# State-space stage: decays from ScalarE with a bias, the next batch's angles made early, two heads' values side by side, the batch loop unrolled

## The chip, the cores and the metric

The kernel runs on one core of a Trainium2 chip. Its time is device microseconds of that core. A core has TensorE (matmul, called PE; its weight loads are PEld), VectorE (DVE), ScalarE (ACT), GpSimd (POOL) and SyncE (SP), which issues DMAs. TensorE's clock has two levels here, 1.2 and 2.4 GHz; a row that says PEclk gives the mean share of 2.4 GHz that was granted.

## The reference

The program is a network of four layers, each `x = x + s * silu(g)`. Only the sequence mixer `s` of the last layer is touched, a state-space model with 8 sequences (batches) of 512 positions, 128 channels, 4 heads of 64 values and a state of 128. Cut to what matters:

```
z, x, Bg, Cg, dd_dt, dd_A, trap, angles = split(u @ W_in)
a  = min(-softplus(dd_A), -1e-4);  dt = softplus(dd_dt + dt_bias)
theta = cumsum(angles[:, :, None, :] * dt[..., None], axis=1)
K = rope(rmsnorm(Bg) * B_norm_w + B_bias, theta)      # per head
Q = rope(rmsnorm(Cg) * C_norm_w + C_bias, theta)
beta = sigmoid(trap);  ell = cumsum(a * dt)
y[i] = sum over j <= i of (Q[i] . K[j]) * exp(ell[i] - ell[j]) * weight(beta, dt)[j] * x[j]   # the chunked sum, whole
y = (y + D * x) * silu(z)
return y @ W_out
```

## The kernel before, in words

The stage is `ssm_phase`. It holds one batch (512 columns of `XN`, channels on partitions) at a time and runs the eight batches one after the other. Each engine has a program of its own; what orders them are semaphores, and within an engine the order is the written one. `i` is the batch, `h` the head, `jk` one of four blocks of 128 keys; the part of a head's 512x512 matrix with queries at or after block `jk` is 512, 384, 256 and 128 columns wide, packed by `KEYS_AT` into three rows of 512 columns (`dec`, `aw`, and banks 0 to 2 of `ps`).

For one batch, TensorE projects B and C (banks 0 and 1), the angles (bank 2) and B and C with their rotated halves swapped (banks 3 and 4); `out(i - 1)` makes the result of the batch before from `y`; then come the means of squares for the norms (`cst("mean")`, banks 5 and 6), the gate z (bank 7, twice) and the values x (banks 5 and 6, L2351). ScalarE squares (L2424), copies the angles out (L2427), takes logarithm and exponential for the norms (L2431, L2433), sine and cosine of the angles (L2435 to L2438), the values out of PSUM, adds the heads' biases (`biased`, L2449) and makes the gates. VectorE multiplies the angles by dt (L2515), sums them along the sequence (L2517), brings them within one turn (five instructions, L2520 to L2531), and norms (L2537, L2539).

Then the four heads. `spread(h)` (TensorE, L2363) copies cosine and sine of head h to the partitions that need them, banks 3 and 4. `prepare(h)` (VectorE) makes the two halves of the rotation, tiles `t2` and `t3` (L2553, L2555), and then the exponents of the decays, `dec = min(ellb - column, 0)`, in four instructions (L2564). `turned(h)` (GpSimd, L2478) adds the halves into `kq`. ScalarE takes the exponential of `dec` in place (L2462), and GpSimd multiplies the four diagonal blocks with a mask that holds the weights, `mm` (L2501; GpSimd makes `mm` at the start of each batch, L2487 and L2493). `products(h)` (TensorE, L2374) makes the 512x512 products Q.K in banks 0 to 2; `weigh(h)` (VectorE) multiplies them with `dec` into `aw` (L2577, L2580); `outputs(h)` (TensorE, L2383) multiplies the values with `aw` into banks 5 and 6, heads 0 and 2 into partitions 0 to 63, heads 1 and 3 into 64 to 127. After the last head VectorE multiplies with the gates into `y` (L2595).

Both `kq` and `dec` have two buffers, `t2`, `t3`, `th` and the PSUM banks one. `turned(h)` must be done before `prepare(h + 1)` overwrites `t2`; `products(h)` waits until `weigh(h - 1)` has read the banks. SP loads per head a row of dt into `dtb` and a row of ell into `ellb`, both broadcast, once the last batch's are used.

## Time and profile before

| | |
|---|---|
| median of 3 runs (lowest, highest) | 3991.99 us (3991.32, 3994.94) |
| the profiled execution, its time | 3988.56 us |
| its span | 3986.8 us |
| busy share of the span, PE, DVE, ACT, POOL | 67%, 62%, 44%, 27% |
| the stage, from VectorE's first instruction (L2508) to the copy of the last result (L2415) | 3503.05 to 3969.4 us |
| granted TensorE clock over the whole execution | 0.799 |

The busy shares are those of the whole network. Only the stage's 466 us, 12% of the span, are touched, so what counts is read there: who waits for whom within one batch.

### The profile page before, as it was taken

To read this page: it belongs to the slowest core of one execution; us is meant where nothing else is said; L and a number is where in the kernel's file an instruction comes from. 1 tells how busy PE (TensorE), PEld (TensorE's weight loads), DVE (VectorE), ACT (ScalarE), POOL (GpSimd) and SP (SyncE) were. 2 spreads that over 40 slices of the span, in tenths; PEclk is the share of its full clock that TensorE was granted. 3 is DMA by queue.
4 is the path that set the end of the run, shared out by engine and by line. 5 is a ranking of instruction groups with operands and counts; after the bars stand their busy time and mean duration, and the time that the engine had idled before them with its cause. 6 is when DMAs were issued, how large, how long until landed. Compare 5 with 4: busy or idle time off the path is not lost. (4 is left out here: it accounts for less than half of the span.)

```text
span 3986.8 us, 45163 instructions
## 1 busy us (share of the span) xinstructions
PE 2677.1 (67%) x10570; PEld 1177.4 (30%) x10570; DVE 2460.7 (62%) x6180; ACT 1769.7 (44%) x2952; POOL 1066.4 (27%) x1279
## 2 busy tenths in 40 slices
PE   4544444534588639935899988767658776667776
PEld 1111334411232226612333333222221111233333
DVE  4787699973645443214565555576459997267776
ACT  3443333314565402225121137644459997543443
POOL 0122465510144217810000024400001111056553
PEclk8766555556798858767899989989869999788898
DMA  2112754121585232321211114200021111000000
GB/s 101 42 42 72 156 90 87 30 59 52 147 125 103 46 97 36 39 68 55 48 29 28 32 32 84 57 0 0 4 74 37 37 37 26 13 28 26 24 16 34
DMA packets 341757, 210.72 MB, mean 53 GB/s; under 512 B 162009, under 2 KB 327689, under 8 KB 340874
## 3 DMA queue, kind: packets, MB, share of 16 engines
q1 hardware_dynamic: 296850, 181.75, 18.5%
q0 software_dynamic: 27904, 25.46, 4.0%
q10 hardware_dynamic: 16896, 2.36, 0.4%
q8 instruction: 33, 0.54, 0.1%
q14 instruction: 74, 0.61, 0.1%
...
## 5 line engine op out<-in xcount | busy, mean ns | idle before, releaser
L2095 ACT ACTIVATE ca_pw<-ca_ps,ca_mx 128x512 f32<-128x512 f32 x512 | 345.6, 686 | 52.4 <-DVE ca_mx L2121 48.6
L2121 DVE TENSOR_REDUCE ca_mx<-ca_ps 128x1 f32<-128x512 f32 x512 | 320.3, 681 | 15.1 <-PE ca_ps L2051 13.1
L1927 DVE CUSTOM_DVE_ANT_0 mx_sums<-mx_ps,w_cst 128x512 f32<-128x512 f32 (+3 forms) x512 | 220.4, 486 | 153.1 <-PE mx_ps L1905 153.1
L2051 PE MATMUL ca_ps<-ca_qs,ca_ks 128*128 128x512 bf16 x512 | 188.3, 404 | 97.1 <-ACT ca_pw L2095 74.0
L1884 PE MATMUL gm_ps<-gm_h,w_w2f 128*128 128x512 f32 x512 | 245.4, 612 | 0.0
L1705 ACT ACTIVATE ta_pw<-ta_ps,w_cst 128x1280 f32<-128x1280 f32 x128 | 166.3, 1326 | 124.5 <-PE ta_ps L1631 118.8
L1705 ACT ACTIVATE at_pw<-at_ps 128x1280 f32<-128x1280 f32 x128 | 153.8, 1236 | 60.7 <-PE at_ps L1631 60.6
L1746 POOL MEMSET at_qs<- 128x2048 bf16 x4 | 7.0, 1806 | 638.2 <-POOLq L36 638.2
L1794 DVE TENSOR_TENSOR ta_pw<-ta_pw,w_cst 128x384 f32<-128x384 f32 x128 | 76.5, 606 | 139.4 <-ACT ta_pw L1705 138.4
L2040 POOL DMA_DIRECT2D GX<-ca_osb x128 | 64.7, 505 | 345.3 <-DVE ca_osb L2113 341.8
L1959 ACT ACTIVATE gm_h<-gm_ps,w_w2f 128x512 f32<-128x512 f32 x64 | 44.0, 688 | 253.1 <-PE gm_ps L1884 253.1
L550 PE MATMUL ex_hps<-ex_xgt,ex_w 128*128 128x128 f32 x384 | 92.2, 416 | 74.7 <-ACT ex_xgt L663 74.7
L2065 PE MATMUL ca_o<-ca_pw,ca_vs 128*32 128x512 f32 x1024 | 140.0, 619 | 0.0
L2374 PE MATMUL ss_ps<-ss_kq 128*128 128x512 f32 (+3 forms) x256 | 99.2, 543 | 58.5 <-DVE ss_aw L2577 47.9
L2051 PEld LDWEIGHTS ca_ps<-ca_qs,ca_ks 128*128 128x128 bf16 x512 | 43.2, 97 | 310.3 <-ACT ca_pw L2095 254.8
L1794 DVE TENSOR_TENSOR at_pw<-at_pw,w_cb_f 128x384 f32<-128x384 f32 x128 | 72.7, 577 | 94.9 <-ACT at_pw L1705 94.9
L1653 PE MATMUL ta_o<-ta_pw,ta_va 128*32 128x512 f32 (+3 forms) x1024 | 104.9, 509 | 30.7 <-POOL ta_pw L1736 30.5
L2478 POOL TENSOR_TENSOR ss_kq<-ss_t 128x512 f32<-128x512 f32 x64 | 86.7, 1374 | 137.7 <-DVE ss_t L2555 137.7
L1230 ACT ACTIVATE f_h<-f_hps,w_w 128x512 f32<-128x512 f32 x64 | 44.0, 687 | 178.4 <-PE f_hps L1194 178.4
L1254 POOL DMA_INDIRECT Acc<-f_y,f_idx x64 | 109.3, 1707 | 33.2 <-issue 18.3
L1884 PEld LDWEIGHTS gm_ps<-gm_h,w_w2f 128*128 128x128 f32 x512 | 89.3, 189 | 91.7 <-issue 91.7
L1653 PE MATMUL at_o<-at_pw,at_va 128*32 128x512 f32 (+3 forms) x1024 | 95.7, 471 | 25.2 <-POOL at_pw L1736 25.2
...
## 6 DMA issues: line engine op xcount, KB each, us to landing
...
```

Source lines behind the costliest of these rows:

```text
L550: last = pe.matmul(hps[:, e % EG, s, :], w1[:, e, s, :], xgt[:, e, :], start=True, stop=True)
L1254: g.indirect_dma_start(Acc, bass.IndirectOffsetOnAxis(ap=idx[:, e, c:c + 1], axis=0), y[:, e % 2, c, :], None, compute_op=ALU.add).then_in ...
L1653: last = pe.matmul(O[32 * a:32 * a + 32, g % 2, jk * 128:T], va[:, jk, h].rearrange("p d x -> p (d x)"), pw[:, h % BUF, at:at + n], start= ...
L1705: act.activation(pw[:, h % BUF, 0:SPAN], ps[:, h % 2, 0:SPAN], ACT.Exp if softmax else ACT.Square, scale=SC[0], bias=0.0 if softmax else c ...
L1794: v.tensor_tensor(three, three, keep.unsqueeze(1).to_broadcast([128, 3, 128]), keeping).then_inc(HD["kept3"][h], 1)
L1884: last = pe.matmul(mps[:, f, :], W(("h1", "h2")[n - 2])[:, j * 512 + f * 128:j * 512 + (f + 1) * 128], src[:, j, :], start=(j == 0), stop= ...
L1927: last = v.tensor_tensor_reduce(out=sums[:, u, at:at + n], in0=ps[:, u, at:at + n], in1=cst("down")[:, T - n:T], scale=-1.0, scalar=3.0e38 ...
L2051: pe.matmul(ps[:, jk, :], ks[:, h // GH % 2, h % GH, jk * 128:(jk + 1) * 128], qs[:, h // GH % 2, h % GH, :], start=True, stop=True).then_ ...
L2065: pe.matmul(O[32 * (h % GH):32 * (h % GH) + M, g % 2, :], vs[:, h % BUF, jk, :], pw[:, h % BUF, jk, :], start=False, stop=last, skip_group ...
L2095: act.activation(pw[:, h % BUF, jk, :], ps[:, jk, :], ACT.Exp, bias=mx[:, h, jk:jk + 1], accum_out=z[:, h, jk:jk + 1]).then_inc(U["exp"][j ...
L2121: v.tensor_reduce(mx[:, h, jk:jk + 1], ps[:, jk, :], AX.X, ALU.max, negate=True).then_inc(U["top"][jk], 1)
L2374: last = pe.matmul(ps[:, at // T, at % T:at % T + n], kq[:, h % 2, K_, jk * 128:(jk + 1) * 128], kq[:, h % 2, Q_, jk * 128:T], start=True, ...
```

## The change

The stage is rearranged in these parts.

1. **Decays.** VectorE no longer makes the exponents. It makes `low`, the smaller of `ellb` and the column on the four diagonal blocks alone (one instruction of 128x512). ScalarE makes each decay in one go, exp(ellb - column), with minus the column as its bias (a fourth plane of `COL`): seven activations a head in place of three.
2. **Buffers.** `aw` is gone: `weigh` writes over `dec`, which has three buffers that go round over heads and batches. `th` and `dtb` have two buffers.
3. **Angles.** Those of batch i + 1 are projected (bank 7), copied, multiplied by dt and summed while batch i is in its last heads; the five instructions to one turn stand on VectorE between `weigh(3)` and `y`. The swapped projections (banks 3 and 4) of batch i + 1 are made between `products(3)` and the last outputs.
4. **Outputs** of heads 0 and 1 are made together, block by block, and those of heads 2 and 3.
5. **Order.** The means stand in front of `out(i - 1)` and now wait for `y`; ScalarE copies the result out after the norms' exponential, not ahead of the logarithm. TensorE reads `XN` for the values, so the copy `xs` is gone.
6. **Loop.** The batch loop is written out eight times on all engines. Rows of ell are loaded head by head, each with its own semaphore.

The core of the diff:

```diff
-            v.tensor_copy(COL[:], cps[:]).then_inc(S["col"], 1)
-            v.wait_ge(S["col"], 1)
+            v.tensor_copy(COL[:, 0:3], cps[:]).then_inc(S["col"], 1)
+            v.tensor_scalar(COL[:, 3], cps[:, 0], -1.0, None, ALU.mult).then_inc(S["col"], 1)
+            v.wait_ge(S["col"], 2)
...
+    DB = 3
...
+        dtb, ellb, low = sb("dtb", 2, T), sb("ellb", H, T), sb("low", 2, NB, 128)
...
-        kq, dec, aw = sb("kq", 2, 2, T), sb("dec", 2, 3, T), sb("aw", 2, 3, T)
+        kq, dec = sb("kq", 2, 2, T), sb("dec", DB, 3, T)
...
+            for i in range(B):
+                if i >= 2:
+                    sp.wait_ge(S["at"], i - 1)
                 for h in range(H):
-                    sp.dma_start(dtb[32 * h:32 * h + 32, :], Rd[0, bass.ds(i * H + h, 1), :].to_broadcast([32, T])
-                                 ).then_inc(S["rows"], 16)
-                    sp.dma_start(ellb[:, h, :], Rd[1, bass.ds(i * H + h, 1), :].to_broadcast([128, T])
-                                 ).then_inc(S["rows"], 16)
+                    sp.dma_start(dtb[32 * h:32 * h + 32, i % 2, :], Rd[0, i * H + h:i * H + h + 1, :].to_broadcast([32, T])
+                                 ).then_inc(R["dt"][i % 2], 16)
+                for h in range(H):
+                    sp.wait_ge(HD["dec"][h], i)
+                    sp.wait_ge(HD["low"][h], i)
+                    sp.dma_start(ellb[:, h, :], Rd[1, i * H + h:i * H + h + 1, :].to_broadcast([128, T])
+                                 ).then_inc(HD["ell"][h], 16)
...
+            def angles(i):
+
+                pe.wait_ge(S["z1sb"], i)
+                project(i, 7, W("in")[:, 768:896]).then_inc(S["ang"], 1)
+
+            def turned(i):
+
+                pe.wait_ge(HD["t2"][H - 1], i)
+                project(i, 3, W("in_turned")[:, 0:128])
+                project(i, 4, W("in_turned")[:, 128:256]).then_inc(S["turn"], 1)
 
             def out(i):
 
                 pe.wait_ge(S["yz"], i + 1)
+                pe.wait_ge(S["angsb"], min(i + 2, B))
...
-                project(i, 2, W("in")[:, 768:896]).then_inc(S["ang"], 1)
-                project(i, 3, W("in_turned")[:, 0:128])
-                project(i, 4, W("in_turned")[:, 128:256])
-                if not first:
-                    out(i - 1)
+                if first:
+                    turned(i)
                 pe.wait_ge(S["sq"], i + 1)
+                pe.wait_ge(S["yz"], i)
                 for n in range(2):
                     last = pe.matmul(ps[:, 5 + n, :], cst("mean"), sq[:, n, :], start=True, stop=True)
                 last.then_inc(S["ms"], 1)
+                if not first:
+                    out(i - 1)
                 pe.wait_ge(S["s"], i)
+                if first:
+                    pe.wait_ge(S["angsb"], 1)
...
-                def outputs(h):
-                    pe.wait_ge(HD["a"][h], i + 1)
-                    r = slice(64 * (h % 2), 64 * (h % 2) + 64)
+                def outputs(pair):
+
+                    for h in pair:
+                        pe.wait_ge(HD["a"][h], i + 1)
                     for jk in range(NB):
                         at, n = KEYS_AT[jk], T - 128 * jk
-                        last = pe.matmul(ps[r, 5 + h // 2, jk * 128:T], xt[:, jk, h * 64:(h + 1) * 64],
-                                         aw[:, h % 2, at // T, at % T:at % T + n], start=False, stop=(jk == NB - 1),
-                                         skip_group_check=True)
-                    last.then_inc(HD["y"][h], 1)
+                        for h in pair:
+                            r = slice(64 * (h % 2), 64 * (h % 2) + 64)
+                            last = pe.matmul(ps[r, 5 + h // 2, jk * 128:T], xt[:, jk, h * 64:(h + 1) * 64],
+                                             dec[:, (i * H + h) % DB, at // T, at % T:at % T + n], start=False,
+                                             stop=(jk == NB - 1), skip_group_check=True)
+                            if jk == NB - 1:
+                                last.then_inc(HD["y"][h], 1)
...
-                for h in range(H):
-                    products(h)
-                    if h:
-                        outputs(h - 1)
-                    if h + 2 < H:
-                        spread(h + 2)
-                outputs(H - 1)
+                products(0)
+                spread(2)
+                products(1)
+                spread(3)
+                products(2)
+                outputs((0, 1))
+                if i + 1 < B:
+                    angles(i + 1)
+                products(3)
+                if i + 1 < B:
+                    turned(i + 1)
+                outputs((2, 3))
...
+            def angles(i):
+                act.wait_ge(S["ang"], i + 1)
+                act.wait_ge(S["th"], i)
+                act.activation(ang[:], ps[:, 7, :], ACT.Copy).then_inc(S["angsb"], 1)
...
-                act.wait_ge(S["ang"], i + 1)
-                act.wait_ge(S["th"], i)
-                act.activation(ang[:], ps[:, 2, :], ACT.Copy).then_inc(S["angsb"], 1)
-                if not first:
-                    finish(i - 1)
...
+                if not first:
+                    finish(i - 1)
...
-                    act.wait_ge(HD["dd"][h], i + 1)
-                    for g, n in ((0, T), (1, T), (2, 256)):
-                        last = act.activation(dec[:, h % 2, g, 0:n], dec[:, h % 2, g, 0:n], ACT.Exp)
+
+                    act.wait_ge(HD["ell"][h], 16 * (i + 1))
+                    act.wait_ge(HD["low"][h], i + 1)
+                    act.wait_ge(HD["y"][(h + 1) % H], i + 1 if h >= DB else i)
+                    for jk in range(NB):
+                        at, n = KEYS_AT[jk], T - 128 * jk
+                        g, o = at // T, at % T
+                        fall = COL[:, 3, jk, i * H + h:i * H + h + 1]
+                        last = act.activation(dec[:, (i * H + h) % DB, g, o:o + 128], low[:, h % 2, jk, :], ACT.Exp, bias=fall)
+                        if n > 128:
+                            act.activation(dec[:, (i * H + h) % DB, g, o + 128:o + n], ellb[:, h, (jk + 1) * 128:T], ACT.Exp,
+                                           bias=fall)
                     last.then_inc(HD["dec"][h], 1)
-
-            turn(0, True)
-            with act.Fori(1, B) as i:
-                turn(i, False)
+                    if h + 2 == H and i + 1 < B:
+                        angles(i + 1)
...
-                v.tensor_copy(xs[:], XN[:, bass.ds(i * T, T)]).then_inc(S["xs"], 1)
...
+            def one_turn(i):
+                now = th[:, i % 2]
                 v.wait_ge(S["th"], i + 1)
...
+            add_angles(0)
+            one_turn(0)
+            for i in range(B):
                 v.wait_ge(S["rs"], i + 1)
+                v.wait_ge(S["turn"], i + 1)
...
+                    v.wait_ge(HD["ell"][h], 16 * (i + 1))
                     if h >= 2:
-                        v.wait_ge(HD["a"][h - 2], i + 1)
-                    for jk in range(NB):
-                        at, n = KEYS_AT[jk], T - 128 * jk
-                        last = v.tensor_scalar(dec[:, h % 2, at // T, at % T:at % T + n], ellb[:, h, jk * 128:T],
-                                               COL[:, 0, jk, bass.ds(i * H + h, 1)], 0.0, ALU.subtract, ALU.min)
-                    last.then_inc(HD["dd"][h], 1)
+                        v.wait_ge(HD["dec"][h - 2], i + 1)
+                    else:
+                        v.wait_ge(HD["dec"][h + 2], i)
+                    v.tensor_tensor(low[:, h % 2], ellb[:, h, :].rearrange("p (j x) -> p j x", j=NB),
+                                    COL[:, 0, :, i * H + h:i * H + h + 1].to_broadcast([128, NB, 128]),
+                                    ALU.min).then_inc(HD["low"][h], 1)
...
-                        last = v.tensor_tensor(aw[:, h % 2, g, o:o + 128], ps[:, g, o:o + 128], dec[:, h % 2, g, o:o + 128],
+                        last = v.tensor_tensor(dec[:, (i * H + h) % DB, g, o:o + 128], ps[:, g, o:o + 128], dec[:, (i * H + h) % DB, g, o:o + 128],
...
+                    elif i + 1 < B:
+                        add_angles(i + 1)
                     weigh(h)
 
+                if i + 1 < B:
+                    one_turn(i + 1)
```

What this moves on the engines is seen in the order of their instructions. First TensorE, from the products of head 2 to the end of a batch. In the rows, L2374 is `products`, L2383 `outputs`. Before:

```order
L2374 MATMUL ss_ps<-ss_kq 128x512
L2374 MATMUL ss_ps<-ss_kq 128x384
L2374 MATMUL ss_ps<-ss_kq 128x256
L2374 MATMUL ss_ps<-ss_kq 128x128
L2383 MATMUL ss_ps<-ss_aw,ss_xt 64x512
L2383 MATMUL ss_ps<-ss_aw,ss_xt 64x384
L2383 MATMUL ss_ps<-ss_aw,ss_xt 64x256
L2383 MATMUL ss_ps<-ss_aw,ss_xt 64x128
L2374 MATMUL ss_ps<-ss_kq 128x512
```

After, in the same place, L2393 is `products`, L2405 `outputs`, L2327 `project`:

```order
L2393 MATMUL ss_ps<-ss_kq 128x128
L2405 MATMUL ss_ps<-ss_dec,ss_xt 64x512 x2
L2405 MATMUL ss_ps<-ss_dec,ss_xt 64x384 x2
L2405 MATMUL ss_ps<-ss_dec,ss_xt 64x256 x2
L2405 MATMUL ss_ps<-ss_dec,ss_xt 64x128 x2
L2327 MATMUL ss_ps<-XN,w_w3a 128x512
L2393 MATMUL ss_ps<-ss_kq 128x512
L2393 MATMUL ss_ps<-ss_kq 128x384
L2393 MATMUL ss_ps<-ss_kq 128x256
L2393 MATMUL ss_ps<-ss_kq 128x128
L2327 MATMUL ss_ps<-XN,w_w3a 128x512 x2
L2405 MATMUL ss_ps<-ss_dec,ss_xt 64x512 x2
```

The outputs of heads 0 and 1 now stand together between the products of heads 2 and 3, with the projection of the next angles behind them, and two more projections stand ahead of the last outputs.

ScalarE, the last two heads of a batch. Before, L2449 is `biased(3)` and L2462 the exponentials of heads 2 and 3:

```order
L2449 ACTIVATE ss_tb<-ss_bc,w_w3a 128x512 x2
L2462 ACTIVATE ss_dec<-ss_dec 128x512 x2
L2462 ACTIVATE ss_dec<-ss_dec 128x256
L2462 ACTIVATE ss_dec<-ss_dec 128x512 x2
L2462 ACTIVATE ss_dec<-ss_dec 128x256
```

After, from the last rows of head 2's exponentials on (L2499 the diagonal blocks, L2501 the rest), L2448 is the copy of the next batch's angles:

```order
L2501 ACTIVATE ss_dec<-ss_ellb,COL 128x128
L2499 ACTIVATE ss_dec<-ss_low,COL 128x128
L2448 ACTIVATE ss_ang<-ss_ps 128x512
L2499 ACTIVATE ss_dec<-ss_low,COL 128x128
L2501 ACTIVATE ss_dec<-ss_ellb,COL 128x384
L2499 ACTIVATE ss_dec<-ss_low,COL 128x128
L2501 ACTIVATE ss_dec<-ss_ellb,COL 128x256
L2499 ACTIVATE ss_dec<-ss_low,COL 128x128
L2501 ACTIVATE ss_dec<-ss_ellb,COL 128x128
L2499 ACTIVATE ss_dec<-ss_low,COL 128x128
```

The copy, which waits for TensorE's projection, now stands in front of head 3's exponentials.

VectorE, from the last head to the next batch's norms. Before, the start of a batch (which follows `y` of the one before) read:

```order
L2511 COPY ss_xs<-XN 128x512
L2513 REGISTER_ALU
L2514 REGISTER_ALU
L2515 TENSOR_TENSOR ss_ang<-ss_ang,ss_dtb 128x512
L2517 SCALAR_TENSOR_TENSOR ss_th<-w_cst,ss_ang 128x512
L2520 TENSOR_SCALAR ss_th<-ss_th 128x512
L2523 TENSOR_SCALAR ss_th<-ss_th 128x512
L2525 SCALAR_TENSOR_TENSOR ss_th<-ss_th 128x512
L2528 SCALAR_TENSOR_TENSOR ss_th<-ss_th 128x512
L2531 TENSOR_SCALAR ss_th<-ss_th 128x512
L2537 SCALAR_TENSOR_TENSOR ss_bc<-ss_ps,w_w3a,ss_sq 128x512
```

After, from the last row of `weigh(3)` (L2625) to the first of the norms (L2586):

```order
L2625 TENSOR_TENSOR ss_dec<-ss_ps,ss_dec 128x128
L2565 TENSOR_SCALAR ss_th<-ss_th 128x512
L2568 TENSOR_SCALAR ss_th<-ss_th 128x512
L2570 SCALAR_TENSOR_TENSOR ss_th<-ss_th 128x512
L2573 SCALAR_TENSOR_TENSOR ss_th<-ss_th 128x512
L2576 TENSOR_SCALAR ss_th<-ss_th 128x512
L2647 TENSOR_TENSOR ss_y<-ss_ps,ss_zs 128x1024
L2586 SCALAR_TENSOR_TENSOR ss_bc<-ss_ps,w_w3a,ss_sq 128x512
```

The five instructions to one turn have moved from behind `y` (L2647) to in front of it; the product and the sum along the sequence have moved further up, ahead of `weigh(3)`.

## Rows read from the trace of the kernel before

**Rows 1.** Stretch, length, busy PE, PEld, DVE, ACT, POOL (count), PEclk: the stage.

```profile
3503.00:3970.00 467.00, 359.73 (x912) 169.62 (x912) 343.40 (x593) 203.65 (x287) 258.06 (x288) 0.89 0.07 23
```

**Rows 2.** By line, L2595 (`y`): duration ns min/median/max, first and last start.

```profile
L2595 DVE TENSOR_TENSOR ss_y<-ss_ps,ss_zs x8: 1223/1224/1225, 3563.6 to 3965.5; 128x1024 f32<-128x1024 f32 x8
```

**Rows 3.** Timeline, TensorE, batch 4: start, us, what, idle before and its releaser.

```profile
3740.61 1.88 PE L2344 MATMUL ss_ps<-ss_sq,w_cst 128*128 128x512 f32 x4
...
3750.15 3.52 PE L2363 MATMUL ss_ps<-ss_th,w_cst 128*128 128x512 f32 x4 [4.09 <-DVE ss_th L2543]
...
3759.29 2.42 PE L2374 MATMUL ss_ps<-ss_kq 128*128 128x512 f32 x8 [0.88 <-POOL ss_kq L2478]
...
3767.83 3.90 PE L2374 MATMUL ss_ps<-ss_kq 128*128 128x512 f32 x8 [3.70 <-DVE ss_aw L2577]
...
3778.03 2.37 PE L2383 MATMUL ss_ps<-ss_aw,ss_xt 128*64 128x512 f32 x8
...
3807.98 3.33 PE L2363 MATMUL ss_ps<-ss_th,w_cst 128*128 128x512 f32 x4 [4.09 <-DVE ss_th L2543]
```

**Rows 4.** Timeline, VectorE, the same batch.

```profile
3749.62 0.43 DVE L2543 TENSOR_SCALAR ss_th<-ss_th 128x512 f32<-128x512 f32 x1 [0.49 <-ACT ss_th L2438]
3753.77 0.69 DVE L2553 SCALAR_TENSOR_TENSOR ss_t<-ss_ps,ss_tb 128x512 f32<-128x512 f32 x1 [3.72 <-PE ss_ps L2363]
...
3756.29 3.30 DVE L2564 TENSOR_SCALAR ss_dec<-ss_ellb,COL 128x512 f32<-128x512 f32 x4
...
3787.93 0.29 DVE L2577 TENSOR_TENSOR ss_aw<-ss_ps,ss_dec 128x128 f32<-128x128 f32 x1 [4.18 <-PE ss_ps L2374]
...
3789.71 0.28 DVE L2577 TENSOR_TENSOR ss_aw<-ss_ps,ss_dec 128x128 f32<-128x128 f32 x1
```

**Rows 5.** Timeline, ScalarE, the same batch.

```profile
3745.32 1.06 ACT L2433 ACTIVATE ss_sq<-ss_sq 128x1024 f32<-128x1024 f32 x1
...
3748.87 0.72 ACT L2438 ACTIVATE ss_th<-ss_th,w_cst 128x512 f32<-128x512 f32 x1
...
3759.62 1.46 ACT L2462 ACTIVATE ss_dec<-ss_dec 128x512 f32<-128x512 f32 x3
```

**Rows 6.** Timeline, GpSimd, the same batch.

```profile
3761.15 1.88 POOL L2501 TENSOR_TENSOR ss_dec<-ss_dec,ss_mm 128x128 f32<-128x128 f32 x4 [1.91 <-ACT ss_dec L2462]
3762.99 2.65 POOL L2478 TENSOR_TENSOR ss_kq<-ss_t 128x512 f32<-128x512 f32 x2
```

**Rows 7.** Groups by line and shape, the stage: busy us, mean ns.

```profile
L2449 ACT ACTIVATE ss_tb<-ss_bc,w_w3a 128x512 f32<-128x512 f32 x64 | 42.5, 712 | 31.7 <-DVE ss_t L2555 31.6
```

**Rows 8.** By line: L2427 (copy of the angles), L2515 (their product with dt).

```profile
L2427 ACT ACTIVATE ss_ang<-ss_ps x8: 591/591/597, 3508.6 to 3910.4; 128x512 f32<-128x512 f32 x8
L2515 DVE TENSOR_TENSOR ss_ang<-ss_ang,ss_dtb x8: 880/1020/1697, 3510.8 to 3911.1; 128x512 f32<-128x512 f32 x8
```

**Rows 9.** L2564 from 3756.8 to 3758 us: the second of four, beside `turned`.

```profile
L2564 DVE TENSOR_SCALAR ss_dec<-ss_ellb,COL x1: 1435/1435/1435, 3756.7 to 3756.7; 128x384 f32<-128x384 f32 x1
```

**Rows 10.** Timeline, VectorE, batch 0, while GpSimd makes `mm`.

```profile
3510.81 1.00 DVE L2515 TENSOR_TENSOR ss_ang<-ss_ang,ss_dtb 128x512 f32<-128x512 f32 x1 [6.15 <-DMA ss_ellb<-Rd]
...
3513.83 1.31 DVE L2520 TENSOR_SCALAR ss_th<-ss_th 128x512 f32<-128x512 f32 x1
...
3517.81 1.63 DVE L2528 SCALAR_TENSOR_TENSOR ss_th<-ss_th 128x512 f32<-128x512 f32 x1
```

**Rows 11.** The page's groups, another stage: four 32-column tiles in turn.

```profile
L2065 PE MATMUL ca_o<-ca_pw,ca_vs 128*32 128x512 f32 x1024 | 140.0, 619 | 0.0
```

**Rows 12.** Timeline, TensorE, two products after idle of 2.3 and 2.6 us.

```profile
3539.51 2.42 PE L2374 MATMUL ss_ps<-ss_kq 128*128 128x512 f32 x8 [2.32 <-POOL ss_kq L2478]
...
3709.99 3.82 PE L2374 MATMUL ss_ps<-ss_kq 128*128 128x512 f32 x8 [2.58 <-POOL ss_kq L2478]
```

**Rows 13.** Busy time by stretch, TensorE alone: `spread(0)` of batch 4.

```profile
3750.15:3753.70 3.55, 3.55 (x5) 0.53 0.00 0
```

**Rows 14.** Timeline, SP's queue, the last of batch 0's eight loads.

```profile
3507.03 0.35 SPq L2315 DMA_DIRECT2D ss_ellb<-Rd  x1
```

More of the change, by code:

```diff
@@ L2291, in ssm_phase @@
     Q_, K_ = 0, 1
+    DB = 3
     with ExitStack() as ctx:
[L2293 to L2295 removed]
+        S = sems(nc, ctx, "ss", "dx bcps ang angsb pj2 xt sq ms std rs norm at th n n1 c1 c2 clamp "
+                 "sin abs cos cosm turn yz sps s z0 z0sb z1 z1sb")
+        R = sems(nc, ctx, "ssr", "dt", 2)
+        HD = sems(nc, ctx, "sh", "ell cps b0 t2 turned qk low dec m1 m2 dm a y", H)
         ps = ctx.enter_context(nc.psum_tensor("ss_ps", [128, 8, T], F32))
         sb = lambda name, *n: ctx.enter_context(nc.sbuf_tensor("ss_" + name, [128, *n], F32))
[L2298 to L2300 removed]
+        zs, bc, rot, dx = sb("zs", 2, T), sb("bc", 2, T), sb("rot", 2, T), sb("dx", 256)
+        sq, xt, ang, th = sb("sq", 2, T), sb("xt", NB, 256), sb("ang", T), sb("th", 2, 3, T)
+        dtb, ellb, low = sb("dtb", 2, T), sb("ellb", H, T), sb("low", 2, NB, 128)
         tb, t2, t3 = sb("tb", 2, T), sb("t2", 2, T), sb("t3", 2, T)
[L2302 removed]
+        kq, dec = sb("kq", 2, 2, T), sb("dec", DB, 3, T)
         mm, own = sb("mm", H, NB, 128), sb("own", NB, 128)
@@ L2459, in turn @@
                         biased(h + 1)
-                    act.wait_ge(HD["dd"][h], i + 1)
-                    for g, n in ((0, T), (1, T), (2, 256)):
-                        last = act.activation(dec[:, h % 2, g, 0:n], dec[:, h % 2, g, 0:n], ACT.Exp)
-                    last.then_inc(HD["dec"][h], 1)
-            turn(0, True)
-            with act.Fori(1, B) as i:
-                turn(i, False)
+                    act.wait_ge(HD["ell"][h], 16 * (i + 1))
[9 more added lines that the diff above has]
+                                           bias=fall)
+                    last.then_inc(HD["dec"][h], 1)
+                    if h + 2 == H and i + 1 < B:
+                        angles(i + 1)
+            angles(0)
+            for i in range(B):
+                turn(i, i == 0)
             finish(B - 1)
@@ L2471, in _ @@
         def _(g):
-            with g.Fori(0, B) as i:
+            for i in range(B):
                 def turned(h):
@@ L2508, in _, with add_angles @@
             v.tensor_tensor(dx[:], W("in")[:, 256:512], W("d_row"), ALU.mult).then_inc(S["dx"], 1)
-            with v.Fori(0, B) as i:
-                v.wait_ge(S["pj2"], i)
-                v.tensor_copy(xs[:], XN[:, bass.ds(i * T, T)]).then_inc(S["xs"], 1)
+            def add_angles(i):
+                now = th[:, i % 2]
                 v.wait_ge(S["angsb"], i + 1)
-                v.wait_ge(S["rows"], 16 * 2 * H * (i + 1))
-                v.tensor_tensor(ang[:], ang[:], dtb[:], ALU.mult).then_inc(S["at"], 1)
+                v.wait_ge(R["dt"][i % 2], 16 * H * (i // 2 + 1))
+                v.tensor_tensor(ang[:], ang[:], dtb[:, i % 2, :], ALU.mult).then_inc(S["at"], 1)
@@ L2529, in _ @@
                                        op0=ALU.mult, op1=ALU.add).then_inc(S["c2"], 1)
                 v.wait_ge(S["c2"], i + 1)
-                v.tensor_scalar(th[:, 0, :], th[:, 0, :], 3.1415925, -3.1415925, ALU.min,
+                v.tensor_scalar(now[:, 0, :], now[:, 0, :], 3.1415925, -3.1415925, ALU.min,
                                 ALU.max).then_inc(S["clamp"], 1)
+            add_angles(0)
+            one_turn(0)
+            for i in range(B):
                 v.wait_ge(S["rs"], i + 1)
+                v.wait_ge(S["turn"], i + 1)
@@ L2580, in weigh @@
                             last = v.scalar_tensor_tensor(
-                                out=aw[:, h % 2, g, o + 128:o + n], in0=ps[:, g, o + 128:o + n],
-                                scalar=COL[:, 1, jk, bass.ds(i * H + h, 1)], in1=dec[:, h % 2, g, o + 128:o + n],
+                                out=dec[:, (i * H + h) % DB, g, o + 128:o + n], in0=ps[:, g, o + 128:o + n],
+                                scalar=COL[:, 1, jk, i * H + h:i * H + h + 1], in1=dec[:, (i * H + h) % DB, g, o + 128:o + n],
                                 op0=ALU.mult, op1=ALU.mult)
@@ L2920, in network @@
             scratch("Rd", [2, B * 4, T], F32)
-            tile(layer, "COL", [128, 3, NB, B * 4], F32)
+            tile(layer, "COL", [128, 4, NB, B * 4], F32)
             ssm_rows_phase(nc, K)
```

53 lines of the change are left out of this document (22 added, 31 removed).

## The prediction, made before the changed kernel was run

> **What bounds the kernel now.** The batch stands whole in front of the next one, so I looked first for its length and then for the chain that sets it. Over the stage no engine is full: in 467 us TensorE is busy 360, VectorE 343, GpSimd 258, ScalarE 204 [rows 1]. So waits bound it, not an engine. `y` starts at 3563.6 in batch 0 and at 3965.5 in batch 7 [rows 2]: seven periods of 57.4 us. The timelines of batch 4 then show where a period goes. From the start of `spread(0)` at 3750.15 to that of the next batch at 3807.98 it is 57.83 us [rows 3]. I measure all that follows from such a start, S.
>
> Three parts. (a) S to the first `t2`, 3.6 us: `spread(0)` alone, 3.52 us for two matmuls that take 1.88 elsewhere [rows 3, 4]; the granted clock was 0.53 there, so mostly the level of 1.2 GHz, after 4.09 us in which TensorE did nothing [rows 3, 13]. (b) The heads, from 3753.77 to the end of `weigh(3)` at 3789.99, 36.2 us [rows 4]. VectorE works through them almost without a pause; the largest is 4.18 us before `weigh(3)`. Of each head's time 3.3 us are the four exponent instructions of L2564 [rows 4]. (c) From there to the next S, 18.0 us: last outputs, projections, `out`, means, logarithm, exponential, sine and cosine, one behind the other.
>
> **The exponents.** `prepare(h)` loses 3.3 us and gains `low`. `low` (128x512, two inputs in SBUF) is not in the trace. Below: half of `y`, which is twice as wide, 0.61 us [rows 2]. Above: L2515, same shape and operands, 1.70 at its worst beside GpSimd [rows 8]. It starts just as `turned(h)` does, as L2564 did. What the two do to each other shows at L2564: its second instruction took 1.44 us beside `turned` [rows 9], more than `y` with 1.22 for over twice the columns. I take 1.0 us.
>
> ScalarE pays. Seven activations of 1280 columns in all replace three that took 1.46 us [rows 5]; that is the bound below. For the bound above: a copy of 512 columns takes 0.59 [rows 8], an exponential of 1024 without a pointer 1.06 [rows 5], so 0.47 per 512 columns and 0.12 fixed; a bias pointer adds 0.71 - 0.59 = 0.12 [rows 7, 8]. Seven times 0.24 and 1.17 for the columns is 2.9. Successive ones overlap a little; I take 2.5, so 1.0 more per head. `dec(h)` to `weigh(h)` is on the path for heads 0 and 3.
>
> **The heads, worked through** (us after S). `spread(0)`: ScalarE now copies the last result after the exponential, so the z projection and the values' matmuls behind it (together three matmuls of 512 columns' worth, 2.8 us at the 1.88 a pair of L2344 [rows 3]) move from 5 us ahead of S to 1 us ahead, and TensorE stands idle about 1 us before S, not 4.09. After 2.32 us of idle a product still took 2.42, after 2.58 us 3.82 [rows 12]. So I take full clock: `t2(0)` starts at 2.0, not 3.6. The gates and `dec(0)` hang on TensorE behind it: `dec(0)` started 9.5 after S [rows 3, 5], now 7.9, done 10.4. Mask 1.9, then `turned(1)` 2.65 [rows 6]: 14.9. `t2(2)` with `t3` takes 2.6 (3753.77 to 3756.29, where L2564 starts) [rows 4]: 17.6; `low` 18.6; `weigh(1)` takes 2.05 (3787.93 to 3789.99 [rows 4]) and needs product 1, which started at 15.0 after a gap like that of 2.58 us, so 3.9: 18.9 to 21.0. `products(2)` waits for it and for `turned(2)` (20.6): 2.4, 23.4. Now the new links: outputs of heads 0 and 1; projection of the angles 0.95 (half of L2344's pair [rows 3]); the copy 0.6 plus start [rows 8]; and behind it on ScalarE, head 3's decays, 2.5, which also wait for outputs(0) since three buffers serve four heads.
>
> The outputs of one head take 2.37 [rows 3], so two in turn 4.6. Side by side is not in this stage. The nearest row is L2065: 1024 matmuls of mean 619 ns (634 us in sum) lie in 140 us of busy time [rows 11], so tiles of 32 columns run at once. I take 2.6 for a pair of 64-column tiles; the bound above is 4.6, doubled at half clock. The Trainium skill (TensorEngine Tiling (Array Packing), Theoretical Speedup) says up to twice as fast for a small dimension of 64, which would give 2.3. The trace has it for 32 columns alone.
>
> So 26.0, 26.95, 27.6, decays 30.1, mask 31.9, `weigh(3)` ends at 34.0, not 39.8. `products(3)`, the product with dt and the sum along the sequence (0.9 to 1.7 and 2) hide in the wait for that mask; without that cover they would cost 3.
>
> **The tail.** `one_turn` now stands between `weigh(3)` and `y`. GpSimd starts on `mm` once the mask of head 3 is done, 2 us earlier, and works on it for 13 us. In batch 0 these instructions met that same work: four took from 3513.83 to 3519.44, 5.6 us [rows 10]; with the fifth 6.0 (at 0.43, as `cosm` of the same shape) to 6.9. I take 6.5. Then `y` 1.22 [rows 2]: 41.75. The means now wait for `y`. The other way to them, pair of outputs 2.6 to 4.1, two projections 1.9, the square 1.0, ends at 39.5 to 41, so it hides behind VectorE. From the means to S: before, 3740.61 to 3750.15, 9.54 [rows 3]. `finish` only changes its place in this chain; 9.55 stays. Next S: 51.3, a period 6.1 shorter than 57.4.
>
> The Trainium skill (SBUF — State Buffer, SBUF: two separate sides) has VectorE and GpSimd hold one port pair in turn, whole instructions long. By that rule each of the five waits for one GpSimd instruction, and 6.5 to 7 us follow, while idle GpSimd would leave 3.2. The trace agrees in [rows 9]: 1.44 us for 384 columns. It speaks against moving them there.
>
> **Edges and free parts.** Batch 0 waited 6.15 us for eight loads, the last issued at 3507.03 [rows 10, 14]; now the four of dt come first, 2 us earlier: -2. The last batch has no angles behind it: `weigh(3)` some 6.5 earlier, its pair of outputs 1 longer than one head's: -5.5. `COL`'s fourth plane, the copy `xs` (beside ScalarE's copy of the angles) and the third buffer are hidden: 0. The loop's end costs nothing visible, so writing it out gives 0.
>
> **Sum** against the profiled 3988.56: 7 x 6.1 = 42.7, 2 and 5.5, together 50 us: 3938.5. The runs' median lies 3.4 above the profiled one: 3942, which I round to 3943.
>
> **Rivals.** (1) TensorE gets the half clock more often, since it now idles 1 to 3 us before the last outputs and before the means: `spread(0)` +1.5, means +1.6, values +1.5, part of them hidden, so +1.5 to +3.5 a batch, 8 batches: 3955 to 3971. For it: 2.58 us of idle was enough [rows 12]. (2) The two heads' outputs don't overlap: +2.0 in front of head 3's decays, +16: 3959. For it: only 32-column tiles are shown. (3) The tail is shorter, `one_turn` 4 us as where it met little of `mm`; then the outputs' way ends last, 1 to 2 less a batch: 3927 to 3935. (4) Slower: from `products(2)` to the angles' projection ScalarE's head-3 decays are held; at half clock (3.9) with outputs in turn (2 x 3.9) and projection (1.8) that is 13.5 for 5.95, +7.6, a period of 58.9: 7 x 1.5, the last batch +1.5, the start -2, about 4002. It decides from 12 us on; the 2.3-us gaps and full clock after them speak against it. (5) The edits change nothing, the instructions that were written out eight times coming late from memory: 3992; no row of the trace speaks for it.
>
> **Chances.** Forecast (3930 to 3955) 0.45; (1) 0.24; (2) 0.10; (3) 0.13; (4) 0.04; (5) 0.04. All but the last two are faster: 0.92, same 0.04, slower 0.04; 0.2% is about what a measurement of this kernel can tell from no change. The range 3918 to 3974 holds the first four with their bounds (`low` 0.6 to 1.7, decays 1.5 to 2.9 twice on the path: 1.5 to 2.5 a batch down, 1.5 up).
>
> **What would show it.** Right: a period of 51 to 52 between starts of `y`; `spread(0)` under 2.2 us; seven activations in 2.4 to 2.6; a pair of outputs under 3; VectorE waiting for GpSimd's mask before `weigh(3)`; `y` starting right behind `one_turn`, and TensorE's means waiting for `y`. Wrong: outputs of 4.6 a pair, `spread(0)` of 3.5, or `y` waiting for the outputs. The sum would be wrong above all if head 3's decays were not what `weigh(3)` waits for, or the gate copies came later than the spread allows.

## The result, and the profile after

The changed kernel takes 3942.34 us (median of 4 runs, 3938.54 to 3949.08) against 3991.85 for the one before (4 runs on the same chip): ratio 0.9876 [0.9859, 0.9893]. The profiled execution took 3941.39 us, its span 3939.7 instead of 3986.8. The stage, from VectorE's first instruction (3500.0) to the end of the last copy (3922.2), shrank from 466.4 to 422.2 us, by 44.2. The other 2.9 us of the span's 47.1 lie outside of it, where nothing was changed. That part varies by itself: one experiment below (the angle copy behind head 3's decays) has a stage of 422.3 in a span of 3950.3. The stage repeated to 0.1 us in the one other profile of this same kernel, so I read small effects from it. The runs' times can't carry them: measured twice, the changed kernel has the ratios 0.9876 and 0.9900 (below), some 10 us apart.

The stage by stretch, columns as in [rows 1]:

```profile
3500.00:3922.20 422.20, 320.61 (x912) 148.74 (x912) 266.99 (x489) 233.53 (x415) 261.16 (x288) 0.91 0.08 25
```

`y`, now L2647, by line, as in [rows 2]:

```profile
L2647 DVE TENSOR_TENSOR ss_y<-ss_ps,ss_zs x8: 1209/1210/1224, 3558.3 to 3916.5; 128x1024 f32<-128x1024 f32 x8
```

VectorE lost 76 us of work and ScalarE gained 30, but no engine is full before or after, so these are not the gain. The gain is in the period: (3916.5 - 3558.3)/7 = 51.2 us between starts of `y`, 57.4 before. (The last `y` now has no turn in front of it, which flatters the first figure; between starts of `spread(0)` it is 51.8 and 57.2.) TensorE from the last pair of outputs of batch 3 to batch 5's means and `out` (columns as in [rows 3]; L2382 is `spread`, L2393 `products`, L2405 a pair of outputs, L2327 projections, L2359 the means, L2345 `out`):

```profile
3708.17 2.37 PE L2405 MATMUL ss_ps<-ss_dec,ss_xt 128*64 128x512 f32 x16 [3.19 <-DVE ss_dec L2625]
...
3715.36 2.57 PE L2359 MATMUL ss_ps<-ss_sq,w_cst 128*128 128x512 f32 x4 [2.90 <-DVE ss_y L2647]
...
3725.70 1.96 PE L2382 MATMUL ss_ps<-ss_th,w_cst 128*128 128x512 f32 x4 [0.87 <-issue]
...
3740.68 3.99 PE L2393 MATMUL ss_ps<-ss_kq 128*128 128x512 f32 x8 [2.62 <-POOL ss_kq L2520]
...
3746.91 2.39 PE L2393 MATMUL ss_ps<-ss_kq 128*128 128x512 f32 x8 [0.52 <-DVE ss_dec L2625]
3749.23 2.38 PE L2405 MATMUL ss_ps<-ss_dec,ss_xt 128*64 128x512 f32 x16
3751.54 1.13 PE L2327 MATMUL ss_ps<-XN,w_w3a 128*128 128x512 f32 x2
3752.50 2.32 PE L2393 MATMUL ss_ps<-ss_kq 128*128 128x512 f32 x8
3754.66 1.88 PE L2327 MATMUL ss_ps<-XN,w_w3a 128*128 128x512 f32 x4
3759.73 3.39 PE L2405 MATMUL ss_ps<-ss_dec,ss_xt 128*64 128x512 f32 x16 [3.19 <-DVE ss_dec L2625]
3763.05 2.61 PE L2327 MATMUL ss_ps<-XN,w_w3a 128*128 128x512 f32 x4
3766.92 1.95 PE L2359 MATMUL ss_ps<-ss_sq,w_cst 128*128 128x512 f32 x4 [1.26 <-DVE ss_y L2647]
3768.71 1.88 PE L2345 MATMUL ss_ps<-ss_y,w_w3a 128*128 128x512 f32 x4
```

`spread(0)` takes 1.96 us after an idle of 0.87, where [rows 3] had 3.5 after 4.09. Sixteen output matmuls of two heads take 2.38, what eight of one head took in [rows 3]. Two things are not as good: after idle of 3.19 us the last pair takes 3.39, and after 2.90 the means of batch 4 take 2.57. The granted clock says what happened, not when it will: behind the same idle of 3.19 us the last pair of batch 3 took 2.37. Over the eight batches the last pair took 3.26 to 4.54 us in six and 2.37 in two (3 and 6). These are four stretches of TensorE alone (start to end, length, busy, PEclk): the last pair, the means of batch 4, the first pair, and the last pair of batch 7, which took 4.54:

```profile
3759.73:3763.05 3.32, 3.32 (x17) 0.68 0.03 5
3715.36:3717.72 2.36, 2.36 (x4) 0.75 0.00 0
...
3749.23:3751.54 2.31, 2.31 (x18) 1.00 0.09 25
...
3911.97:3916.50 4.53, 4.53 (x16) 0.50 0.00 0
```

0.50 is the level of 1.2 GHz throughout, 0.68 and 0.75 a mixture of it and of 2.4 GHz.

VectorE's timeline over the same time (L2556 and L2560 are the angles' product and sum, L2565 to L2576 the turn):

```profile
3727.76 0.69 DVE L2602 SCALAR_TENSOR_TENSOR ss_t<-ss_ps,ss_tb 128x512 f32<-128x512 f32 x1 [2.16 <-PE ss_ps L2382]
...
3730.28 0.68 DVE L2614 TENSOR_TENSOR ss_low<-ss_ellb,COL 128x512 f32<-128x512 f32 x1
...
3753.33 0.69 DVE L2556 TENSOR_TENSOR ss_ang<-ss_ang,ss_dtb 128x512 f32<-128x512 f32 x1 [1.49 <-ACT ss_ang L2448]
3754.06 1.22 DVE L2560 TENSOR_TENSOR_SCAN ss_th<-w_cst,ss_ang 128x512 f32<-128x512 f32 x1
3757.53 0.29 DVE L2625 TENSOR_TENSOR ss_dec<-ss_ps,ss_dec 128x128 f32<-128x128 f32 x1 [2.24 <-POOL ss_dec L2543]
...
3759.50 0.41 DVE L2565 TENSOR_SCALAR ss_th<-ss_th 128x512 f32<-128x512 f32 x1
3759.95 1.38 DVE L2568 TENSOR_SCALAR ss_th<-ss_th 128x512 f32<-128x512 f32 x1
3761.36 1.42 DVE L2570 SCALAR_TENSOR_TENSOR ss_th<-ss_th 128x512 f32<-128x512 f32 x1
3762.81 1.42 DVE L2573 SCALAR_TENSOR_TENSOR ss_th<-ss_th 128x512 f32<-128x512 f32 x1
3764.27 1.37 DVE L2576 TENSOR_SCALAR ss_th<-ss_th 128x512 f32<-128x512 f32 x1
3765.56 1.21 DVE L2647 TENSOR_TENSOR ss_y<-ss_ps,ss_zs 128x1024 f32<-128x1024 f32 x1
```

ScalarE's timeline, the angles' copy and the first and last of head 3's seven activations:

```profile
3752.70 0.60 ACT L2448 ACTIVATE ss_ang<-ss_ps 128x512 f32<-128x512 f32 x1 [5.64 <-PE ss_ps L2327]
3753.19 0.39 ACT L2499 ACTIVATE ss_dec<-ss_low,COL 128x128 f32<-128x128 f32 x1
...
3755.27 0.39 ACT L2499 ACTIVATE ss_dec<-ss_low,COL 128x128 f32<-128x128 f32 x1
```

GpSimd's timeline, head 3's mask:

```profile
3755.74 1.69 POOL L2543 TENSOR_TENSOR ss_dec<-ss_dec,ss_mm 128x128 f32<-128x128 f32 x4 [3.50 <-ACT ss_dec L2499]
```

The chain reads through the four timelines: outputs of heads 0 and 1, the angles' projection, ScalarE's copy at 3752.70, seven activations in 2.47 us (3753.19 to 3755.66), GpSimd's mask, `weigh(3)` at 3757.53 after 2.24 us of waiting, the turn beside GpSimd, `y`, and the means 0.15 us behind `y`.

### The profile page after: what moved, and what is told of

It reads as the page before. It is cut to its first block and busy times, and to the rows that moved or that the text cites. A ratio compares the mean times of both kernels' runs of the same rounds, so it can differ in the third digit from the quotient of the medians.

```text
span 3939.7 us, 44724 instructions
## 1 busy us (share of the span) xinstructions
PE 2622.9 (67%) x10570; PEld 1143.8 (29%) x10570; DVE 2384.4 (61%) x6077; ACT 1798.5 (46%) x3080; POOL 1067.4 (27%) x1279
## 5 line engine op out<-in xcount | busy, mean ns | idle before, releaser
L1653 PE MATMUL ta_o<-ta_pw,ta_va 128*32 128x512 f32 (+3 forms) x1024 | 104.2, 506 | 31.9 <-POOL ta_pw L1736 31.8
L1241 POOL DMA_INDIRECT f_xg<-Xt,f_idx x64 | 74.7, 1167 | 133.8 <-DVE f_idx L1280 114.9
```

The source lines that it names most:

```text
L1653: last = pe.matmul(O[32 * a:32 * a + 32, g % 2, jk * 128:T], va[:, jk, h].rearrange("p d x -> p (d x)"), pw[:, h % BUF, at:at + n], start= ...
```

## The experiments

Unless one says otherwise, each is the changed kernel with one edit. "Stage" and "period" are as above; a ratio is against the kernel before on the same chip. A bracketed change of the stage is against the changed kernel's 422.2 (for the unrolled one, against 466.4).

**Outputs of a pair in turn.**

```diff
-                    for jk in range(NB):
-                        at, n = KEYS_AT[jk], T - 128 * jk
-                        for h in pair:
+                    for h in pair:
+                        for jk in range(NB):
+                            at, n = KEYS_AT[jk], T - 128 * jk
```

> The changed kernel with one thing undone: the outputs of a pair of heads are made one head after the other, not block by block in turn. Theory: the two 64-column tiles run at once (a pair took 2.37 us after the change), and one after the other they take 4.6. The first pair stands in front of the angles' projection and head 3's decays, so weigh(3) ends 2.3 us later; the second pair hides mostly behind VectorE's turn. So 2.3 to 2.7 us a batch: 3960 to 3964 us, ratio to before 0.992 to 0.993. Rival (head 3's decays are not what weigh(3) waits for): no change, 3942.

Measured: 3960.81 us, 0.9937 [0.9921, 0.9954]; stage 434.7 (+12.5), period 53.0. The first pair of a batch on TensorE:

```profile
3755.20 3.93 PE L2405 MATMUL ss_ps<-ss_dec,ss_xt 128*64 128x512 f32 x16
```

3.93 instead of 2.38: side by side is worth 1.55 us a pair, less than twice 2.3, since in turn too the end of one head's matmuls runs beside the start of the other's (matmul by matmul, the second head's first starts 0.8 us before the first head's last ends). From the first `t2` to the end of `weigh(3)` it added 1.4 a batch (33.1 for 31.7), which confirms that this pair stands in front of `weigh(3)`.

**Exponents on VectorE again**, as before the change, but with a fourth `dec` buffer, so that VectorE doesn't wait for outputs. It is compared with four buffers alone, below.

```diff
-                    v.tensor_tensor(low[:, h % 2], ellb[:, h, :].rearrange("p (j x) -> p j x", j=NB),
-                                    COL[:, 0, :, i * H + h:i * H + h + 1].to_broadcast([128, NB, 128]),
-                                    ALU.min).then_inc(HD["low"][h], 1)
+                    for jk in range(NB):
+                        at, n = KEYS_AT[jk], T - 128 * jk
+                        last = v.tensor_scalar(dec[:, (i * H + h) % DB, at // T, at % T:at % T + n], ellb[:, h, jk * 128:T],
+                                               COL[:, 0, jk, i * H + h:i * H + h + 1], 0.0, ALU.subtract, ALU.min)
```

> The changed kernel with four decay buffers and the exponents back on VectorE: four subtract-and-min instructions a head in place of low, and three exponentials without bias on ScalarE. Theory: VectorE has again 3.3 us a head in place of 0.7, and the heads go by it; weigh(3) ends 2.5 to 4 us later a batch, less than the 4 x 2.6 taken out since GpSimd's and TensorE's way stood close behind: 3962 to 3975 us. Rival (the decays were the whole gain): 3985 or more. Rival (they gave nothing): 3942.

Measured: 3975.40 us (9 runs), 0.9954 [0.9938, 0.9971]; stage 449.7, 30.9 above that with four buffers. The decays from ScalarE are the largest single part: 3.3 us a period (2.9 of it between `t2(0)` and the end of `weigh(3)`, 34.6 for 31.7, and 0.6 between the means and `spread(0)`), and 7.6 in the last batch.

**`y` ahead of the turn.** `one_turn(i + 1)` moved from in front of `y` to behind it, nothing else.

> The changed kernel with y placed in front of the five instructions to one turn on VectorE. Theory: these take 6.1 us beside GpSimd's mask work and hold y, and with it the means; without them the means wait for outputs, projections and square, 5.5 us (full clock) to 7 us (half clock) after weigh(3) in place of 7.4. So 0.3 to 1.9 us less in each of 7 batches: 3929 to 3940 us. Rival (the outputs' way ends last anyway, or the turn is then late for the sine): 3942 or up to 3950.

Measured: 3940.69 us, 0.9884 [0.9867, 0.9900]; stage 419.6 (-2.6), period 51.3. Its last pair of outputs and its means:

```profile
3755.70 4.54 PE L2405 MATMUL ss_ps<-ss_dec,ss_xt 128*64 128x512 f32 x16 [3.19 <-DVE ss_dec L2625]
...
3763.85 1.98 PE L2359 MATMUL ss_ps<-ss_sq,w_cst 128*128 128x512 f32 x4 [1.11 <-ACT ss_sq L2457]
```

`y` no longer waits for 6 us of turn, but for outputs of 4.54 us instead of 2.38, behind a TensorE idle of 3.19. Only in one batch (5) was that pair at full clock, and there the means came 5.55 us after `weigh(3)`, not 7.3. In the stretch of the row above the granted clock was 0.50:

```profile
3755.70:3760.10 4.40, 4.40 (x16) 0.50 0.00 0
```

The half clock ate the saving: from start to start of `spread(0)` it is 51.7 us, 51.8 without the edit. Of the 2.6 us off the stage, 2.2 lie in the last batch, which has no turn for `y` to overtake; the edit changes nothing there, but its outputs took 3.81 instead of 4.54 and its `out` 1.98 instead of 3.72.

**Loops written out, alone, on the kernel before** (`for i in range(...)` in place of each `Fori`, nothing else).

> The kernel before with only its batch loops of this stage written out. Theory: the loop's end and the registers cost nothing on the path: 3991.9 us, within 0.2% of before. Rival (the writing out is worth something by itself, 0.2 us at each of seven loop ends and a register step ahead of many instructions): up to 10 us faster. Rival (instructions fetched late): slower.

Measured: 3980.15 us (10 runs), 0.9986 [0.9976, 0.9997]; stage 460.9 (-5.5). TensorE's timeline in its batch 4, the means and `spread(0)`:

```profile
3738.29 1.88 PE L2344 MATMUL ss_ps<-ss_sq,w_cst 128*128 128x512 f32 x4
...
3747.66 3.61 PE L2363 MATMUL ss_ps<-ss_th,w_cst 128*128 128x512 f32 x4 [4.10 <-DVE ss_th L2543]
```

ScalarE's, its copy of the last result, and the same copy in the kernel before:

```profile
3738.49 0.60 ACT L2415 ACTIVATE SX<-ss_ps 128x512 f32<-128x512 f32 x1 [2.78 <-PE ss_ps L2327]
...
3740.98 0.60 ACT L2415 ACTIVATE SX<-ss_ps 128x512 f32 x1 [2.95 <-PE ss_ps L2327]
```

9.37 us from means to `spread(0)`, in batches 1 to 7, for 9.54 in [rows 3]: the copy starts 0.20 us behind the means, 0.37 in the loop. With 0.2 us ahead of batch 0's `spread(0)` that is 1.6 us. The other 3.9 lie mostly between `t2(0)` and `weigh(3)` (35.3 for 35.7 a batch), which varies by 4 us from batch to batch with the clock (0.94 granted over the heads of one batch that took 33.7 us, 0.82 over one of 38.3). So unrolling is worth a little, 1 to 10 us by the interval, not nothing, but only the 1.6 us can be pointed at.

**`out` ahead of the means again.** The two pieces of TensorE's list change places, and the means' own wait for `y` goes.

> The changed kernel with out(i - 1) in front of the means again on TensorE. Theory: out takes 1.8 us and needs y as well, so the means, logarithm, exponential and all behind them start 1.8 us later in seven batches: 3955 us. Rival (the copy of the result before the sine, or the clock, takes it back): 3942 to 3948.

Measured: 3950.71 us, 0.9902 [0.9882, 0.9923]; stage 436.5 (+14.3), period 53.5; the means 9.07 us after `weigh(3)` instead of 7.33. `out`'s 1.7 us lie bare in the chain, as expected, seven times; the last 2 of the 14.3 lie elsewhere. The runs' times show less than the stage: the ratio, 0.9902, is hardly above the changed kernel's own 0.9876 and 0.9900.

**GpSimd's masks wait for the turn** (`g.wait_ge(S["clamp"], i + 1)` ahead of `mm`). VectorE's timeline of the turn and `y` is then:

```profile
3763.84 0.42 DVE L2566 TENSOR_SCALAR ss_th<-ss_th 128x512 f32<-128x512 f32 x1
3764.30 0.43 DVE L2569 TENSOR_SCALAR ss_th<-ss_th 128x512 f32<-128x512 f32 x1
3764.76 0.69 DVE L2571 SCALAR_TENSOR_TENSOR ss_th<-ss_th 128x512 f32<-128x512 f32 x1
3765.49 0.69 DVE L2574 SCALAR_TENSOR_TENSOR ss_th<-ss_th 128x512 f32<-128x512 f32 x1
3766.22 0.43 DVE L2577 TENSOR_SCALAR ss_th<-ss_th 128x512 f32<-128x512 f32 x1
3768.12 1.23 DVE L2648 TENSOR_TENSOR ss_y<-ss_ps,ss_zs 128x1024 f32<-128x1024 f32 x1 [1.47 <-PE ss_ps L2405]
```

> The changed kernel where GpSimd begins the masks of batch i only after VectorE has done that batch's turn. Theory: the two engines hold each other up in SBUF; alone the five instructions take 2.9 us in place of 6.1. Then y waits for the outputs and the means for the square, as with y first: 0.3 to 1.9 us a batch less, 3929 to 3940 us, and the masks (13.6 us) are still ready before the first sum of halves. Rival (the turn takes 6 us for itself): 3942. Rival (the masks come late): slower.

Measured: 3939.42 us, 0.9865 [0.9847, 0.9884]; stage 419.0 (-3.2). The turn takes 2.8 us, 6.1 beside the masks, so the contention is shown. But `y` now waits 1.47 for the outputs, which take 4.0 after 3.0 of idle, and the means start 7.19 us after `weigh(3)`, only 0.14 earlier. TensorE's timeline there:

```profile
3764.08 4.00 PE L2405 MATMUL ss_ps<-ss_dec,ss_xt 128*64 128x512 f32 x16 [3.04 <-DVE ss_dec L2626]
```

Of the 3.2 us off the stage, 0.6 are batch 0's, whose own turn no longer meets the masks, 1.4 the seven periods', and 1.2 the last batch's, which has no turn to shorten.

**Four `dec` buffers, alone** (`DB = 4`).

> The changed kernel with four decay buffers in place of three. Theory: head 3's decays stand behind the copy of the next angles on ScalarE, and that waits for TensorE behind the outputs of heads 0 and 1 anyway; the buffer is not the last thing waited for. So no change: 3942 us. Rival (the third buffer's reuse holds head 3): 1 to 3 us a batch faster, 3918 to 3934. It is also the base that the run with the exponents back on VectorE needs.

Measured: 3944.91 us, 0.9893 [0.9876, 0.9909]; stage 418.8 (-3.4). The heads of batches 0 to 6 take what they took (31.3 to 31.9); in the last, where no angle copy stands in front of head 3's decays, 28.9 instead of 30.3. In the others that copy ends later than the outputs that the fourth buffer frees ScalarE from. The other 2.2 us off the stage lie behind the last `weigh(3)`, where outputs and `out` took 4.06 and 1.98 instead of 4.54 and 3.72.

**Angles at their old place**, behind `y` (projected after B and C, copied after the square, product, sum and turn behind `y`; bank 2 again).

> The changed kernel with the angles at the old place: projected with the batch itself, multiplied, summed and turned behind y. Theory: early angles cost as much as they give. Late, head 3's decays start 1.5 us sooner (no projection and copy ahead of them), and the turn ends after the exponential, holding sine and norms by 1.5 to 3 us: 3940 to 3955 us. Rival (early angles are a main part of the gain, some 3 us a batch): 3965 or more.

Measured: 3947.21 us, 0.9893 [0.9877, 0.9910]; stage 422.6 (+0.4), period 51.6. The heads 30.5, the means 5.55 after `weigh(3)`, but 12.13 from means to `spread(0)`, which then took up to 3.9 us (`t2(0)` 3.86 behind it in four batches). Making the angles early is worth nothing on net: what it takes off the seam, it puts into the heads (the copy) and in front of `y` (the turn).

**The changed kernel again**, beside the next two.

> The changed kernel itself, beside the two below on the same chip, so that they can be compared with it: 3942 us, ratio to before 0.988.

Measured: 3947.74 us, 0.9900 [0.9879, 0.9921]; stage 422.2, period 51.2.

**ScalarE's angle copy behind head 3's decays**, and nothing else.

> The changed kernel with ScalarE's copy of the next angles behind head 3's decays, nothing else moved. Theory: the decays start 1.5 us sooner (they then wait for the outputs of head 0 alone), but VectorE's product and sum of the angles stand ahead of weigh(3) and now wait for the copy: weigh(3) ends 0.3 to 0.8 us sooner a batch, 3936 to 3940 us. Rival (the copy's place is what held weigh(3), all of it): 1.5 us a batch, 3930. Rival (the angles come too late): slower.

Measured: 3946.75 us, 0.9883 [0.9858, 0.9908]; stage 422.3. A miss: nothing moved. VectorE's product with dt still stands ahead of `weigh(3)` and waits for the copy, which now comes later. VectorE's timeline in its batch 4, the product and the start of `weigh(3)`:

```profile
3764.93 0.98 DVE L2556 TENSOR_TENSOR ss_ang<-ss_ang,ss_dtb 128x512 f32<-128x512 f32 x1 [2.86 <-ACT ss_ang L2448]
...
3767.66 0.29 DVE L2625 TENSOR_TENSOR ss_dec<-ss_ps,ss_dec 128x128 f32<-128x128 f32 x1 [0.35 <-POOL ss_dec L2543]
```

**All four together**: four buffers, the copy behind head 3's decays, product and sum behind `weigh(3)`, and `y` ahead of the turn:

```diff
-    DB = 3
+    DB = 4
...
-                    if h + 2 == H and i + 1 < B:
+                    if h + 1 == H and i + 1 < B:
                         angles(i + 1)
...
-                    elif i + 1 < B:
-                        add_angles(i + 1)
                     weigh(h)
...
-                    one_turn(i + 1)
+                    add_angles(i + 1)
...
                 v.tensor_tensor(y[:], ps[:, 5:7, :], zs[:], ALU.mult).then_inc(S["yz"], 1)
+                if i + 1 < B:
+                    one_turn(i + 1)
```

> The changed kernel with four decay buffers, ScalarE's copy of the angles behind head 3's decays, VectorE's product and sum behind weigh(3), and y in front of the turn. Theory: head 3's decays then wait for low alone, and weigh(3) for products(3), 29.1 us after the start of spread(0) in place of 31.9: 2.7 us a batch; the tail gives 0.5 to 1.5 more as in the run with y first. Together 3 to 4 us in seven batches: 3914 to 3922 us. Rival (the turn, beside the masks, ends too late for sine and norms, and takes it back): 3930 to 3942.

Measured: 3911.87 us (3908.44 to 3916.28), 0.9803 [0.9781, 0.9825]; 36 us below the changed kernel on the same chip. Stage 388.3, period 47.1. The stage by stretch, and the stretch of its last outputs in one batch:

```profile
3507.70:3896.00 388.30, 307.20 (x912) 145.05 (x912) 281.63 (x489) 234.29 (x415) 270.68 (x288) 0.94 0.09 28
...
3744.97:3747.20 2.23, 2.23 (x16) 1.00 0.04 7
```

TensorE's timeline there:

```profile
3744.97 2.37 PE L2405 MATMUL ss_ps<-ss_dec,ss_xt 128*64 128x512 f32 x16 [0.52 <-DVE ss_dec L2625]
...
3750.37 1.98 PE L2359 MATMUL ss_ps<-ss_sq,w_cst 128*128 128x512 f32 x4 [1.11 <-ACT ss_sq L2457]
```

The heads take 29.0 instead of 31.7, and the means come 5.55 after `weigh(3)` in every batch, since the outputs ahead of `y`, after 0.5 us of idle, run at full clock (1.00 in the stretch). Alone, the first edit gained 3.4 us of stage, the second nothing, the last 2.6, and nearly all of that in the last batch alone: in the seven others each only moved the wait to the next late piece. What moving product and sum does without the others wasn't tried.

## Why the prediction came out

The mechanism was right in the main, with one term put too low and one rival partly true, and the time was right, but its closeness owes something to chance. The sum said 50 us off the stage; the stage gave 44.2, and the rest of the difference of the medians (49.5) lies outside it or in which runs were drawn: beside the same kernel again, the difference was 41.7. Of the 6 us that the stage fell short, 5 are the seven periods', 1.9 the last batch's, and the start gave 0.9 back. Part of it is a slip of measure: the sum took its 51.3 from S to S, but subtracted it from 57.4, the period between starts of `y`, where S to S was 57.2; that alone is some 1.7 us. From S to S:

| us | predicted | measured |
|---|---|---|
| S to `t2(0)` | 2.0 | 2.06 to 2.58, 3.86 in batch 0; mean 2.5 |
| `t2(0)` to the end of `weigh(3)` | 32.0 | 31.3 to 31.95 |
| from there to the means | 7.7 | 7.33, once 8.46 |
| means to the next S | 9.55 | 9.73 to 10.45; mean 10.1 |
| period | 51.3 | 51.8 |
| gain a period, before less after | 6.1 | 57.2 - 51.8 = 5.4 |
| start, last batch | 2, 5.5 | 2.9, 3.6 |

- **`spread(0)` at full clock: right.** 1.96 us after 0.87 of idle. In batches 1 and 2 `t2(0)` came 2.58 behind it, since the values came late (below). In batch 0, after 4.40 us of idle, `spread(0)` still took 3.75, and `t2(0)` came 3.86 behind. That the later copy of the result is what closed the idle is read from the timeline; no run undid it.
- **Exponents for `low` and seven activations: right in kind.** `low` took 0.68 in all 32 cases, the lower bound's neighbour, not 1.0; it starts some 0.2 us ahead of `turned` (3743.24 and 3743.41 in batch 4) and isn't held by it, as the second instruction of L2564 was [rows 9]. Seven activations took 2.47 (2.5 predicted).
- **Side by side: right.** 2.38, not 2.6. The Trainium skill (TensorEngine Tiling (Array Packing), Theoretical Speedup) has up to two times for 64 columns; the trace agrees, a pair now costs what one head did [rows 3].
- **Head 3's decays and mask as what `weigh(3)` waits for: right**; the wait for the mask is in the row at 3757.53, and the exchange in turn lengthened just this stretch.
- **The turn: right**, 5.98 us from the end of `weigh(3)` to `y`, for 6.5. The Trainium skill (SBUF — State Buffer, SBUF: two separate sides) has one of the two engines hold the shared ports for a whole instruction. The trace agrees in kind: four instructions of 1.37 to 1.42 beside GpSimd, 0.43 to 0.69 when it is held back.
- **"`finish` only changes its place in this chain; 9.55 stays": the term that was off most**, by 0.5 a batch. Ahead of the logarithm the copy lay beside the means; behind the exponential part of it lies bare: 9.73 where all ran at full clock, +0.2. The rest is the clock, at two places. In batches 4 and 7 the means themselves were slow, and the logarithm came 0.6 to 0.7 later. In batches 1 and 2 it was the z projection and the values' matmuls (L2369), which wait for that copy after 2.34 us of idle and now stand right in front of `spread(0)`; TensorE's timeline of batch 1:

```profile
3565.64 1.39 PE L2327 MATMUL ss_ps<-XN,w_w3a 128*128 128x512 f32 x2 [2.34 <-ACT SX L2443]
3566.82 3.36 PE L2369 MATMUL ss_ps<-w_w3a,XN 128*128 128x256 f32 x8
3570.01 1.88 PE L2382 MATMUL ss_ps<-ss_th,w_cst 128*128 128x512 f32 x4
```

  3.36 us for the values, 1.89 in batch 4, and `spread(0)` starts 10.39 after the means. In batches 3, 5 and 6 the values took 1.89 behind the same idle of 2.34.
- **Rival (1), the clock, was partly so**: besides the above, the last outputs took 3.26 us and more in six of eight batches. That mostly hid beside the turn, for which `y` waits longer; it cost 1.1 in batch 2 (means 8.46 behind `weigh(3)`), and the last batch, whose outputs (4.54) and `out` (3.72) stood bare: 3.6 gained there, not 5.5.
- **"Writing it out gives 0"** was wrong by 1.6 us at least. Rivals (2) to (5) did not occur; (2) as an experiment cost 12.5 us, not 16.

The parts don't add. Undone one at a time, they cost 31 (decays), 14 (`out` behind the means), 12.5 (side by side) and 0 us of stage (early angles); unrolling, done alone on the kernel before, gave 1.6 to 5.5. That is some 60 us for 44. Two pieces that end in the same wait each look as if they carried it. Not tried singly: the copy of the result behind the exponential, three `dec` buffers for two, the swapped projections made early, and the order of the loads.
